# First expert layer: from all experts over all tokens to 35 tiles of routed rows with register-addressed weights

## The reference

```python
logits = jnp.einsum('td,ed->te', xt, Wr)
scores = jax.nn.softmax(logits, axis=-1)
k_scores, k_ids = jax.lax.top_k(scores, K)               # K = 2 of E = 8 experts
k_w = k_scores / (k_scores.sum(axis=-1, keepdims=True) + eps)
combine = jnp.sum(jax.nn.one_hot(k_ids, E, dtype=x.dtype) * k_w[..., None], axis=1)
g = jnp.einsum('td,efd->etf', xt, Wg)                    # F = 512
u = jnp.einsum('td,efd->etf', xt, Wu)
h = jax.nn.relu(g) * u
out_e = jnp.einsum('etf,edf->etd', h, Wd)
out = jnp.einsum('te,etd->td', combine, out_e)
```

## Time and profile before

| | |
|---|---|
| Time, three runs | 1590.21 us median (1580.11, 1590.21, 1596.01) |
| The profiled execution's own time | 1580.43 us |
| Its span, first to last instruction | 1578.6 us |
| Mean granted clock of PE | 0.967 |
| PE busy | 1439.2 us (91%) |
| PEld, DVE, ACT, POOL busy | 1109.6, 1027.8, 835.2, 668.8 us |
| First expert layer, from its first matmul to the next stage's | 288.75 to 549.40 us |

### The profile page before, as it was taken

One profiled execution on the slowest core, in us unless ns is written; L12 is line 12 of the kernel. 1 busy time (PEld: TensorE's weight loads), 2 busy tenths in 40 slices (PEclk: granted clock), 3 DMA queues, 4 the chain that ended last, 5 costly groups with the idle time before them and its releaser, 6 DMA issues. The chain is left out here.

```text
span 1578.6 us, 43229 instructions
## 1 busy us (share of the span) xinstructions
PE 1439.2 (91%) x16097; PEld 1109.6 (70%) x16097; DVE 1027.8 (65%) x1711; ACT 835.2 (53%) x1319; POOL 668.8 (42%) x735
## 2 busy tenths in 40 slices
PE   7888998889999987779999999999999999986884
PEld 4445666678998846447777777777777777766774
DVE  4334555578778649567777777777777777738562
ACT  5553332332232237536666666666666666656671
POOL 2300000378778636553344334443444334413763
PEclk9979999999999999979999999999999999998997
DMA  3064996131110010175655566556655565422212
GB/s 83 23 177 130 253 235 145 41 112 64 43 66 23 15 34 2 41 171 135 158 130 129 131 156 141 128 127 148 156 123 128 138 156 134 110 65 82 58 48 87
DMA packets 65765, 170.76 MB, mean 108 GB/s; under 512 B 15072, under 2 KB 37206, under 8 KB 65680
## 3 DMA queue, kind: packets, MB, share of 16 engines
q1 hardware_dynamic: 60688, 154.13, 39.7%
q10 hardware_dynamic: 2688, 11.78, 2.8%
...
...
## 5 line engine op out<-in xcount | busy, mean ns | idle before, releaser
L2015 DVE TENSOR_REDUCE hat_tops<-banks 128x1 f32<-128x500 f32 x672 | 439.3, 676 | 153.9 <-PE banks L1760 153.1
L1888 ACT ACTIVATE hat_pb<-banks 125x896 f32<-125x896 f32 x384 | 340.2, 916 | 221.3 <-PE banks L1779 216.3
L1760 PE MATMUL banks<-hat_kh,hat_qm 128*128 128x500 f32 x672 | 299.1, 464 | 4.3 <-DVE hat_tops L2015 3.3
L1779 PEld LDWEIGHTS banks<-hat_q,hat_k 128*125 128x125 f32 x1536 | 219.8, 189 | 74.1 <-ACT hat_pb L1888 31.8
L1779 PE MATMUL banks<-hat_q,hat_k 128*125 128x224 f32 x1536 | 250.7, 286 | 15.5 <-ACT hat_pb L1888 9.1
L1957 POOL CAST hat_kh<-hat_kf 128x500 fp32r<-128x500 f32 x96 | 58.4, 609 | 399.3 <-ACT hat_kf L1901 384.1
L1770 PE MATMUL banks<-hat_pb,hat_vs 125*27 125x168 f32 (+1 forms) x6144 | 166.9, 261 | 0.1
L1770 PEld LDWEIGHTS banks<-hat_pb,hat_vs 125*27 125x27 f32 (+1 forms) x6144 | 132.0, 98 | 44.0 <-issue 24.3
L1760 PEld LDWEIGHTS banks<-hat_kh,hat_qm 128*128 128x128 f32 x672 | 128.4, 193 | 43.5 <-DVE hat_tops L2015 28.9
L1325 ACT ACTIVATE ffn_rg<-banks 128x448 f32<-128x448 f32 x128 | 69.7, 545 | 162.8 <-PE banks L1258 162.7
L1963 POOL TENSOR_TENSOR hat_kl<-hat_kf,hat_kh 128x500 fp32r<-128x500 f32 x96 | 119.5, 1272 | 1.4 <-DMA hat_k<-hat_kh 1.4
...
## 6 DMA issues: line engine op xcount, KB each, us to landing
hat_k<-hat_kh SPq DMA_DIRECT2D x256, 187.5 KB, 4.7
...
hat_k<-hat_kl SPq DMA_DIRECT2D x128, 187.5 KB, 4.5
...
```

The source lines that it names most:

```text
L1760: peak_out.inc(nc.tensor.matmul(g.bank(PK + m % 2)[:, 0:SB], qm[u][:].rearrange("p h i -> p (h i)")[:, r * 128:r * 128 + 128], kh[u][:, c ...
L1779: mm = nc.tensor.matmul(g.bank(2 * (t % 2) + j // 2)[0:SW, (j % 2) * QW:(j % 2 + 1) * QW], k3[u][:, j, t * SW:(t + 1) * SW], q3[u][:, j, : ...
L1888: exped.inc(nc.scalar.activation(pb[t % 6][:].rearrange("p (n i) -> p n i", n=2), g.ps[0:SW, 2 * (t % 2):2 * (t % 2) + 2, 0:2 * QW], ACT.E ...
L2015: peaked.inc(v.tensor_reduce(tops[:, r, n:n + 1], g.bank(PK + m % 2)[:, 0:SB], AX_X, ALU.max))
```

## The change

`experts0` computes only chosen pairs of token and expert. 2 x 1792 pairs fill at most 35 tiles of 128 rows, each of one expert, and always 35 are computed; lanes without a pair hold zeros or old rows and are not sent back.

- All 24 weight matrices (8 experts x 3) are loaded, split and kept in SBUF before the first tile: `up_high`, `up_low` (each 128 by 8192) and `down_both`, which has high and low columns side by side. SP loads them through a ring of six buffers. POOL makes the high parts of the first six, ACT those of the other 18; POOL makes 17 low parts and DVE seven, three between choosing and laying out the rows and four after naming them.
- Normalisation no longer makes the high and low parts of x. PE transposes the normalised x to rows, ACT copies them out and SP stores them in DRAM.
- The routing is that of `Dispatch`, moved up in the file, with other bases: each expert's rows begin at a tile's start. `deal` computes each tile's expert, as an offset into the weights.
- POOL clears the row tiles, then fetches tile t + 8 and sends tile t, 35 of each.
- A tile t on PE: transpose of its rows, six up matmuls with x stationary and 512 weight columns moving, four transposes of the gated product, and twelve down matmuls, three for each quarter, with the hidden part stationary and 128 columns of `down_both` moving, all into one sum of 128 columns. Up and down each begin with a load of the tile's offset from SBUF into a register of PE (`value_load`).
- ACT and DVE: high and low parts of x, relu and gate of 512 columns, high and low parts of the transposed product, the copy of the result. ACT also makes 28 share matrices.
- At the end SP loads both results of each token from `token_rows0`, and PE and DVE join and add them as in `experts1`.

```diff
-class Ahead:
...
+class Dispatch(Choice):
...
+        self.lanes, self.lane_row = g.spare[:, 1, :].bitcast(BF16).rearrange("p (n i) -> p n i", i=128), sb("lane_row", [128, 128], BF16)
...
-def experts_relu(g, ahead):
...
-                        for n in range(2):
-                            mm = three(g.bank(4 + 2 * (j % 2) + n)[:, 0:CW], wh[u][:, n, f128], wl[u][:, n, f128], chunk(xh, c), chunk(xl, c))
-                        up_out.inc(mm)
-                        if j >= LAG:
-                            down(e, u, j - LAG)
-                        elif later(e):
-                            down(e - 1, 1 - u, UN - LAG + j)
...
+def experts0(g):
...
+    TILES, RAWS, SPLIT, OUTS, AHEAD = 2 * TT + E - 1, 6, 6, 4, 8
+    SETS = 3 * E
+    DVE_FIRST, DVE_LAST = (8, 9, 10), (20, 21, 22, 23)
+    BY_POOL = [k for k in range(SETS) if k not in DVE_FIRST + DVE_LAST]
+    BY_DVE = DVE_FIRST + DVE_LAST
+    GROUPS = [(0, 4), (4, 8), (8, 12), (12, 14)]
...
+                for k in range(SETS):
+                    e, m = divmod(k, 3)
+                    if k >= RAWS:
+                        sp.wait_ge(*w_low_of(k - RAWS))
+                    source = g.d[("FWgT", "FWuT", "FWdT")[m]][e]
+                    sp.dma_start(raw_part(k), source if m < 2 else source.rearrange("(f p) d -> p f d", p=128)).then_inc(raw_in[k % RAWS], 16)
+                    if k == 12:
+                        for i, (a, b) in enumerate(GROUPS):
+                            sp.wait_ge(rows_kept, i + 1)
+                            sp.dma_start(g.rows[a * 128:b * 128].rearrange("(t p) d -> p t d", p=128), rows[:, a:b, :]).then_inc(rows_stored, 16)
+                sp.wait_ge(rows_stored, 16 * len(GROUPS))
+                for u in range(OUTS):
+                    sp.wait_ge(out_sent[u], 16 * ((TILES - u + OUTS - 1) // OUTS))
+                for i, (a, b) in enumerate(GROUPS):
+                    for k in range(2):
+                        source = g.token_rows0[k * NT + a * 128:k * NT + b * 128].rearrange("(t p) d -> p t d", p=128)
+                        sp.dma_start(back[i][k], source).then_inc(back_in[i], 16)
...
+                nc.gpsimd.memset(rows[:], 0.0).then_inc(cleared, 1)
+
+                def subtract(k):
+                    pool.wait_ge(*w_high_of(k))
+                    nc.gpsimd.tensor_tensor(low_part(k), raw_part(k), high_part(k).bitcast(F32), ALU.subtract).then_inc(w_low_pool, 1)
+
+                for k in range(SPLIT):
+                    pool.wait_ge(raw_in[k % RAWS], 16)
+                    pool.sem_inc(rounding, 1)
+                    nc.gpsimd.tensor_copy(high_part(k), raw_part(k)).then_inc(w_high_pool, 1)
+                    subtract(k)
+                for k in BY_POOL[SPLIT:]:
+                    subtract(k)
+
+                def fetch(t):
+                    nc.gpsimd.indirect_dma_start(out=rows[:, t, :], out_offset=None, in_=g.rows, in_offset=bass.IndirectOffsetOnAxis(ap=pick.fetch_id[:, t:t + 1], axis=0),
+                                                 bounds_check=NT - 1, oob_is_err=False).then_inc(rows_in[t], 16)
+
+                def send(t):
+                    pool.wait_ge(out_kept, t + 1)
+                    nc.gpsimd.indirect_dma_start(out=g.token_rows0, out_offset=bass.IndirectOffsetOnAxis(ap=pick.send_id[:, t:t + 1], axis=0),
+                                                 in_=ow[t % OUTS][:], in_offset=None, bounds_check=2 * NT - 1, oob_is_err=False).then_inc(out_sent[t % OUTS], 16)
+
+                pool.wait_ge(rows_stored, 16 * len(GROUPS))
+                pool.wait_ge(pick.named, 2)
+                for t in range(AHEAD):
+                    fetch(t)
+                for t in range(TILES):
+                    if t + AHEAD < TILES:
+                        fetch(t + AHEAD)
+                    send(t)
...
+                norm.on_pe(pe, lambda c: pick.on_pe_logits(g.bank(4), (0, 3, 7, 10)[c], (3, 7, 10, TT)[c]))
+                for i, (a, b) in enumerate(GROUPS):
+                    if i == 3:
+                        pe.wait_ge(rows_kept, 1)
+                    for t in range(a, b):
+                        mm = nc.tensor.transpose(g.bank(i % 3)[:, (t - a) * D:(t - a + 1) * D], g.xn[:, t * 128:t * 128 + 128], c_["ident"])
+                    mm.then_inc(rows_out, 1)
+                pe.wait_ge(norm.logged, CH)
+                pe.wait_ge(rows_kept, len(GROUPS))
+                pick.on_pe_tally(pe, g.bank(3))
+                pick.on_pe_places(pe, g.bank(2))
+                pick.on_pe_list(pe, g.bank(3))
+                pe.wait_ge(pick.named, 2)
+                pe.wait_ge(dealt, 1)
+
+                def weights_of(t):
+                    return pe.value_load(expert[0:1, t:t + 1], min_val=0, max_val=(E - 1) * 2 * F)
+
+                def turn(t):
+                    pe.wait_ge(rows_in[t], 16)
+                    if t:
+                        pe.wait_ge(x_low, t)
+                    nc.tensor.transpose(g.bank(6)[:, 0:128], rows[:, t, :], c_["ident"]).then_inc(turned, 1)
+
+                def up_part(t):
+                    at = weights_of(t)
+                    pe.wait_ge(x_low, t + 1)
+                    if t >= 2:
+                        pe.wait_ge(made, t - 1)
+                    for n in range(2):
+                        out = g.bank(2 * (t % 2) + n)
+                        wide = bass.ds(at + n * F, F)
+                        nc.tensor.matmul(out, xh[t % 2][:], up_high[:, wide], start=True, stop=False, skip_group_check=True)
+                        nc.tensor.matmul(out, xl[t % 2][:], up_high[:, wide], start=False, stop=False, skip_group_check=True)
+                        mm = nc.tensor.matmul(out, xh[t % 2][:], up_low[:, wide], start=False, stop=True, skip_group_check=True)
+                    mm.then_inc(up, 1)
+
+                def turn_h(t):
+                    pe.wait_ge(made, t + 1)
+                    if t >= 2:
+                        pe.wait_ge(low, t - 1)
+                    for f in range(FT):
+                        mm = nc.tensor.transpose(g.bank(4 + t % 2)[:, f128(f)], hf[t % 2][:, f128(f)], c_["ident"])
+                    mm.then_inc(h_out, 1)
+
+                def down_part(t):
+                    at = weights_of(t)
+                    pe.wait_ge(high, t + 1)
+                    pe.wait_ge(low, t + 1)
+                    if t:
+                        pe.wait_ge(out_kept, t)
+                    for f in range(FT):
+                        nc.tensor.matmul(g.bank(7)[:, 0:128], hh[t % 2][:, f128(f)], down_both[:, bass.ds(at + f * 256, 128)], start=(f == 0), stop=False, skip_group_check=True)
+                        nc.tensor.matmul(g.bank(7)[:, 0:128], hh[t % 2][:, f128(f)], down_both[:, bass.ds(at + f * 256 + 128, 128)], start=False, stop=False, skip_group_check=True)
+                        mm = nc.tensor.matmul(g.bank(7)[:, 0:128], hl[t % 2][:, f128(f)], down_both[:, bass.ds(at + f * 256, 128)], start=False, stop=(f == FT - 1), skip_group_check=True)
+                    mm.then_inc(down, 1)
...
+                turn(0)
+                pe.wait_ge(w_low_pool, len(BY_POOL))
+                pe.wait_ge(w_low_dve, len(BY_DVE))
+                for t in range(TILES):
+                    if t + 1 < TILES:
+                        turn(t + 1)
+                    up_part(t)
+                    if t >= 1:
+                        turn_h(t - 1)
+                    if t >= 2:
+                        down_part(t - 2)
+                turn_h(TILES - 1)
+                down_part(TILES - 2)
+                down_part(TILES - 1)
+                pe.wait_ge(lots_made, 2)
+                pe.wait_ge(made, TILES)
+                for i, (a, b) in enumerate(GROUPS):
+                    pe.wait_ge(back_in[i], 32)
+                    for t in range(a, b):
+                        for k in range(2):
+                            mm = nc.tensor.matmul(g.bank(i)[:, (t - a) * 128:(t - a + 1) * 128], back[i][k][:, t - a, :], lots[k][:, t, :],
+                                                  start=(k == 0), stop=(k == 1))
+                    mm.then_inc(joined, 1)
...
+                for k in range(SPLIT, 11):
+                    cast(k)
+                pick.on_act_tally(act, g.bank(3))
+                for k in range(11, 14):
+                    cast(k)
+                pick.on_act_marks(act)
+                for k in range(14, SETS):
+                    cast(k)
...
+                keep_high(0)
+                for t in range(TILES):
+                    if t + 1 < TILES:
+                        keep_high(t + 1)
+                    rectify(t)
+                    if t >= 1:
+                        round_up(t - 1)
+                    if t == 3:
+                        act.wait_ge(pick.shared, 1)
+                    if 3 <= t < 3 + 2 * TT:
+                        k, n = divmod(t - 3, TT)
+                        mul = nc.scalar.activation(lots[k][:, n, :], c_["ident"], ACT.Copy, scale=pick.share[:, k, n:n + 1])
```

(34 more changed lines are left out.)

503 lines of the change are left out of this document (200 added, 303 removed).

## The result

| | before | changed |
|---|---|---|
| Time, median (range, runs) | 1585.53 us (1580.11 to 1596.01, 4) | 1514.78 us (1506.34 to 1519.04, 4) |
| Ratio | | 0.954, 95% interval 0.9465 to 0.9614 |
| The profiled execution's own time and span | 1580.43, 1578.6 | 1506.34, 1504.5 |
| Mean granted clock of PE | 0.967 | 0.944 |

The change makes the kernel 4.6% faster; the forecast of 1513 us was 2 us off, and the range held. But two errors of 6 and 9 us worked against each other in it, so the stage is read alone first. The PE timeline of the changed kernel answers to the earlier trace rows: the stage begins with the first matmul of the layer's normalisation, and the next one begins at 476.79.

A forecast was written before the change was run, and what follows sets the result against it. PE's matmul columns bound the layer. First up product at 338.5, plus 114 for tiles, 3, 4 and 17.4, put the next stage at 478.6 instead of 549.4: -70.8, sum 1509.6, forecast 1513 us, range 1495 to 1572.

The forecast's parts named there:

- The tile: PE's work on one tile: up 1.38, transposes 0.55, down 1.32, together 3.25 us; 35 tiles 114 us.
- the router row: Earlier trace's router matmuls, 8 columns after a full load, about 0.11 us apart; taken as the down matmuls' spacing.
- rival of a two-pass rate: Narrow down matmuls run at the two-pass rate, 0.22 us each: +46 us, 1559; chance 0.10.
- Register loads: Two loads per tile from SBUF into a PE register, each put below 1 us and at nothing on the path.
- the cover: Matmuls already handed to the array hide PE's register loads; semaphores fire 1.3 to 1.9 us before matmuls are due.
- rival of partly bare loads: PE's register loads show 0.3 to 1.2 us each, 70 times: +21 to +84 us, 1534 to 1595; chance 0.16.
- Ahead of the tiles: Routing and layout before the tile loop: first fetch at 334 us, between 329 and 341; first up product at 338.5.
- DVE beside POOL: Slower DVE operations beside POOL's subtractions while rows are laid out: 0 to 11.4 us, taken as 5.
- The clock: PE starts the tile loop at half clock after standing idle; half of about 8 us, so +4 us.
- the 3 us put for what is not covered: At the loop's end, the last tile's gate, high part and remainder are not covered: +3 us.
- After the tiles: Copy, send, fetching back, joining matmuls and addition after the last down product: 17.4 us, then the switch to the next stage.
- rival of tiles bound by hand-overs: Tiles wait 0.5 to 1 us each for bank 6 or DVE's order: +18 to +35 us, 1531 to 1548; chance 0.07.

The follow-up runs named there:

- static_address: Changed kernel with program constants in place of PE's 70 register loads of weight addresses: 3.252 us per tile, next stage 4.3 us earlier.
- loads_doubled: Changed kernel with each of the 70 parts loading its address twice: 4.63 us per tile, +1.28, the stage 42 us longer.
- lows_on_dve: Changed kernel with six weight subtractions moved from POOL to DVE, behind the names: comparisons 4.64 instead of 10.95 us, first fetch 6.3 us earlier, stage 179.9 us.
- warm: Changed kernel with added matmuls on constants, read by nobody, where PE waits: stage 182.0 us, a gain of 1.4 us.

## Why the forecast held, point by point

The working on record against the trace, in us from the stage's start:

| step | forecast | measured | off |
|---|---|---|---|
| start to the last chunk of xn | 12.1 | 12.2 | +0.1 |
| chunk to first fetch | 33.2 | 35.9 | +2.7 |
| first fetch to first up product | 4.5 | 5.4 | +0.9 |
| first up product to the end of the last down product | 121.0 | 122.4 | +1.4 |
| from there to the next stage | 19.1 | 19.6 | +0.5 |
| sum | 189.9 | 195.6 | +5.7 |

**The tile: right.** 3.25 us from rows of other matmuls; the array's own time, without the loads, is 3.25. The down matmuls stand 0.11 apart, as the router row said. By the Trainium skill's 81 ns for a pair ("TensorE: Matmul & The Clock Gate", section "Back-to-back issue gap") the tile would have been 0.36 us shorter; the trace has 0.111 and decides against it. The rival of a two-pass rate (0.22) is out.

**Register loads: the price right, the cover wrong.** The load itself is 0.30 us, with its register work and check 0.64 us of the queue, below the 1 us taken. The step that failed is the cover, "1.3 to 1.9 us": it counted when semaphores fire, not how far ahead of the array the queue runs. Over twelve down matmuls the array takes 1.34 us and the queue about 0.95 (eight address operations of 0.12), so that the queue gains some 0.4 us there, less than the 0.64 of a load, and all its work together comes to 3.3 us per tile; the lead ahead of an up product is about one load's worth. `static_address` puts what shows at 0.1 us per tile, 3.3 us in the loop (0.05 per load, where the rival of partly bare loads began at 0.3; its upper end of 1.2 makes 1597 us, not 1595), and `loads_doubled` shows the cliff behind it: every further load is bare. The Trainium skill ("DMA: Bandwidth & Descriptors", section "Latency and other measured facts") has about 600 ns as the floor of a tensor_load; the trace has 300 ns for the load, and 640 for all that comes with it.

**Ahead of the tiles: right in kind, too small in size.** DVE beside POOL was the term with the widest bounds (0 to 11.4) and was taken at 5. The lane comparisons alone lost 6.3 (`lows_on_dve`), and four further operations of 0.2 to 0.3 took 1.1 to 1.3 us elsewhere in the chain, so about 10 us where 5 were taken (an estimate from these rows). The first fetch was only 2.7 us late, so the rest of the chain was some 2.5 us shorter than its model in the later layer; which operations saved that was not looked into. Overlooked besides were the transpose of the second tile, which stands ahead of the first up product and waits for the second fetch (333.76, 1.35 us behind the first one's), and the first register load, which has nothing to hide behind.

**The clock: taken at twice its size.** "+4" at the loop's start, from 8 us at half clock, was 1.7 by `warm`: the clock rose 3.8 us after the first up product. The 2.3 us that were given away this way paid for most of what the loads show in the loop, 3.3 us where nothing was put, so the +1.4 of this row is small by luck in part. The fourth tile's up product, 4.30 us behind the third's for want of DVE's `ffn_hf`, adds 1.0: six small operations for the shares (1.5 us of DVE, 341.6 to 343.3) stand ahead of that. The end was forecast well: PE's work from the last up product's start (1.38 for it, 8 transposes at 0.11, three down products at 1.34) and the 3 us put for what is not covered make 9.3 us, and it took 8.8, with the last down product at half clock (0.21 apart) behind a wait of 0.6 us for bank 7.

**After the tiles: right.** 16.4 us from the last down product's end to the end of the last addition, where 17.4 was forecast; the switch to the next stage took 3.2 instead of 1.7.

**Handing over: right.** The loop's waits for another engine are 1.4 us in all, so the rival of tiles bound by hand-overs is out, and POOL's 2.6 us per tile never bound, not even at 2.83.

**The sum came out by luck in part.** +5.7 in the stage met -7.5 ahead of it and -1.5 behind it. The stretch ahead has nothing of the change in it. The waits of PE in the profile before, 228 to 290 us:

```profile
PE banks L850 <- DMA ctx_cx<-ctx: 5.0, 3, 2.0
PE banks L250 <- PEq L2695: 1.6, 1, 1.6
```

In the changed kernel's profile the first of these is absent, which accounts for 5.0 of the 7.5 us. In the second profile of the same changed kernel the last chunk of xn ends at 305.1 instead of 293.4, in the other runs anywhere between 293.4 and 304.6, while the stage agrees to 0.4 us. This second profile has no such DMA wait either; of its 11.7 us 8.5 were lost before 117 us, with a granted clock of 0.54 against 0.66 from 50 to 100 us. So these 7.5 us are scatter from run to run, of DMA waits and of the clock, not the change. Four later executions of the changed kernel have their median at 1521.79 us, 9 above the forecast, and are 62 us faster than the kernel before beside them, where the first four were 71 faster. What the change alone brought is best put at the 65 us of the stage.
